# Last stage of a four-stage kernel: one block in place of two, rows kept apart from the bias adds, and two groups' column products issued ahead of the column weights

## The reference, cut to what matters

```python
def _L1_ffn_ref(x, col_emb, gate_w1, gate_b1, gate_w2, gate_b2, W_cols, b_cols, proj_w, proj_b, ln_g, ln_b):
    similarity = jnp.einsum('bsd,cd->bsc', _l2norm(x), _l2norm(col_emb))
    h = jax.nn.gelu(x @ gate_w1 + gate_b1, approximate=False)
    gate_values = jax.nn.sigmoid(h @ gate_w2 + gate_b2)
    logits = similarity + gate_values
    k = max(1, int(C * SPARSITY))                 # k = 1
    _, top_idx = jax.lax.top_k(logits, k)
    mask = jnp.sum(jax.nn.one_hot(top_idx, C, dtype=logits.dtype), axis=-2)
    weights = mask * jax.nn.softmax(logits, axis=-1)
    cols = jax.nn.gelu(jnp.einsum('bsd,cdn->bscn', x, W_cols) + b_cols, approximate=False)
    cols = cols * weights[..., None]
    combined = cols.reshape(Bq, Sq, -1)
    y = combined @ proj_w + proj_b + x
    mu = jnp.mean(y, axis=-1, keepdims=True)
    var = jnp.mean((y - mu) ** 2, axis=-1, keepdims=True)
    return (y - mu) * jax.lax.rsqrt(var + 1e-05) * ln_g + ln_b
...
x = x + jnp.tanh(g_ffn[1]) * _L1_ffn_ref(_layernorm(x, axis=-1), ...)
```

## Time and profile before

| | us |
|---|---|
| median of three runs (lowest to highest) | 1504.93 (1501.84 to 1507.17) |
| the profiled execution's own time | 1506.88 |
| its span from the first to the last instruction | 1505.1 |
| PE, DVE, ACT, POOL busy in the span | 1360.8, 1015.7, 620.0, 546.7 |
| last stage: first transposes of the gating start | 1184.8 |
| sigmoid starts, weights' transposes start | 1236.2, 1246.7 |
| second block's first matmul | 1252.9 |

### The profile page before, as it was taken

The page is one execution under the profiler, slowest core; times in us unless marked ns, Lnnn a source line. Parts: engine busy times, 40 slices in busy tenths (PEclk is TensorE's granted clock), DMA queues, the critical chain, the costliest instruction groups (busy, mean ns, idle before and its releaser), DMA issues. The chain is left out here.

```text
span 1505.1 us, 33126 instructions
## 1 busy us (share of the span) xinstructions
PE 1360.8 (90%) x12672; PEld 963.5 (64%) x12672; DVE 1015.7 (67%) x1961; ACT 620.0 (41%) x1371; POOL 546.7 (36%) x829
## 2 busy tenths in 40 slices
PE   3687999999999984899999999999999687999997
PEld 3464677777777762567776777667776463555555
DVE  6777665677556764778888888778888543444544
ACT  4433212211221112656666666656666442222221
POOL 0576888888840004323222232222231570000000
PEclk9998999999999996899999999999999688999999
DMA  8205445454531008667667777666672000000000
GB/s 243 66 1 171 132 134 165 124 165 133 162 110 41 32 1 117 123 83 95 84 85 92 97 96 91 84 83 84 84 93 24 0 1 0 13 12 12 20 17 25
DMA packets 92774, 120.25 MB, mean 80 GB/s; under 512 B 7414, under 2 KB 78899, under 8 KB 90348
## 3 DMA queue, kind: packets, MB, share of 16 engines
q1 hardware_dynamic: 83436, 87.82, 34.5%
q0 software_dynamic: 9216, 30.73, 7.0%
HBM read 96.42 MB, written 22.10 MB: 79 GB/s over the span
## 5 line engine op out<-in xcount | busy, mean ns | idle before, releaser
L1123 DVE TENSOR_REDUCE s_neg_max<-banks 112x1 bf16<-112x487 f32 x512 | 323.7, 662 | 92.5 <-PE banks L1234 89.3
L1059 ACT ACTIVATE s_prob<-banks 128x448 f32<-128x448 f32 x512 | 265.9, 547 | 180.2 <-PE banks L1256 180.0
L640 DVE TENSOR_TENSOR s_m<-banks,s_base 128x512 f32<-128x512 f32 x256 | 164.6, 685 | 129.3 <-PE banks L794 129.1
L1234 PE MATMUL banks<-s_k_t,s_q_t 96*112 96x487 bf16 x512 | 198.5, 388 | 1.5 <-DVE s_neg_max L1123 1.5
L1256 PEld LDWEIGHTS banks<-s_q_t,s_k_t 112*128 112x128 bf16 x2048 | 143.4, 99 | 82.1 <-issue 33.9
L1256 PE MATMUL banks<-s_q_t,s_k_t 112*128 112x112 bf16 x2048 | 187.2, 214 | 3.7 <-issue 3.0
L794 PE MATMUL banks<-s_gate_sel,s_tw 64*128 64x256 f32 x1024 | 147.4, 408 | 0.9 <-DVE s_m L640 0.8
L1270 PE MATMUL banks<-s_prob,s_v 128*32 128x112 f32 (+1 forms) x4096 | 129.2, 265 | 7.7 <-issue 7.7
L834 PE MATMUL banks<-s_m,s_act_t 128*112 128x256 f32 x512 | 129.8, 389 | 5.9 <-DVE x_res L659 5.8
L817 PEld LDWEIGHTS banks<-s_x_t,s_m 128*128 128x128 f32 x1024 | 119.1, 192 | 21.2 <-issue 20.9
L817 PE MATMUL banks<-s_x_t,s_m 128*128 128x112 f32 x1024 | 130.5, 281 | 0.0
(11 more groups left out here) (257 smaller groups left out, 2182.7 us busy)
## 6 DMA issues: line engine op xcount, KB each, us to landing
k_parts<-s_k_split POOLq DMA_DIRECT2D x64, 281.2 KB, 3.4
s_k_t<-k_parts SPq DMA_DIRECT2D x32, 562.5 KB, 7.7
s_tw<-in_tw SPq DMA_DIRECT2D x16, 1024.0 KB, 5.1
s_k_raw<-in_ctx_k POOLq DMA_DIRECT2D x64, 187.5 KB, 3.6
s_k_t<-k_parts SPq DMA_DIRECT2D x32, 375.0 KB, 9.9
s_v_raw<-in_ctx SPq DMA_DIRECT2D x32, 256.0 KB
s_src<-in_ctx SPq DMA_DIRECT2D x8, 896.0 KB, 14.4
s_k_t<-k_parts SPq DMA_DIRECT2D x32, 187.5 KB, 11.2
```

The lines of the kernel that those rows point to most:

```text
L640: nc.vector.tensor_tensor(dst[:, :, :, rows_], got, base[:, :, rows_].unsqueeze(2).broadcast_to([P, 2, B, HR]), ALU.add).then_inc(S["merge ...
L1059: nc.scalar.activation(prob[t % 2][:, c, :], w.bank(SCORE + n % SRING, P, TILE), ACT.Exp, scale=DH ** -0.5).then_inc(S["exp_done"], 1)
L1123: nc.vector.tensor_reduce(neg_max[half][:, ROWS + h, 0:1], w.bank(MAX + n % MRING, T, NKEY), AX.X, ALU.max, negate=True).then_inc(S["max_d ...
L1234: nc.tensor.matmul(w.bank(MAX + n % MRING, T, NKEY), q_t[k][0:ROWS, h, :], k_t[k][0:ROWS, h, FIRST:FIRST + NKEY], start=True, stop=True).t ...
```

## The change

`stage4` becomes one block with one set of semaphores, and the gating's loop over the groups is written out eight times.

- **Rows.** The norm writes straight to `xn`, which holds all 32 batches, and waits for nothing of POOL. POOL adds `proj_b` in `xn` in place, once PE has transposed the batch. Its adds of `ln_b` to `x_res` come after all of these: batches 0 to 15 at once, 16 to 31 once the weights are done.
- **Order at the start.** The norm's own root comes first, the columns' norm after the first group; the root of the columns is taken before the first group's PSUM copies on ACT, the copy of the columns' transposes goes from ACT to DVE, and the scaling of `ln_g` and `ln_b` comes after the second group's norm.
- **Two groups ahead.** After the gating PE computes the column products of groups 0 and 1 without their weights, over four banks for the Gelus (`ahead`); ACT writes the Gelu to `weighted`. The weights' transposes come group by group (`weights`), between the products of group 1, each with the spread of one turn of group 0. DVE multiplies in place (`weigh_ahead`). Then PE spreads group 1's weights, with the output of group 0 between, and groups 2 to 7 run as before.
- **Weights.** The softmax's factor (`total`, 32 values per partition) is split into three bf16 parts instead of the 512 weights, and one multiplication by the mask makes all parts.

```diff
+            @block.gpsimd
+            def _(pool):
+                pool.wait_ge(w.columns_in, N_COLUMNS)
+                for b in range(B):
+                    wait(pool, "x_tr", b + 1)
+                    nc.gpsimd.tensor_tensor(xn[:, b, :], xn[:, b, :], proj_b[:], ALU.add).then_inc(S["kept"], 1)
+                wait(pool, "biased", 1)
+                for b in range(B):
+                    if b == B // 2:
+                        wait(pool, "wts_done", 1)
+                    wait(pool, "xn_done", b + 1)
+                    nc.gpsimd.tensor_tensor(w.x_res[:, b, :], w.x_res[:, b, :], ln_b[:], ALU.add).then_inc(S["x_biased"], 1)
...
             @block.scalar
+                evacuate(0)
+                wait(act, "radicand_done", 3)
+                nc.scalar.activation(root[:], sumsq[:], ACT.Sqrt).then_inc(S["root_done"], 1)
+                nc.scalar.activation(table[:], cgate1_b[:], ACT.Gelu)
...
+                nc.scalar.activation(logit[:], logit[:], ACT.Exp).then_inc(S["soft_done"], 1)
+                nc.scalar.activation(table[:], cgate1_b[:], ACT.Gelu)
+                def ahead_gelu(g, j):
+                    wait(act, "ahead_ps", J4 * g + j + 1)
+                    nc.scalar.activation(weighted[g][:, j, :], w.bank(AHEAD_BANKS[j % 4], P, GT), ACT.Gelu,
+                                         bias=b_cols[:, j:j + 1]).then_inc(S["ahead_gelu"], 1)
+                for j in range(J4):
+                    ahead_gelu(0, j)
+                for g in range(0, NG, 2):
+                    wait(act, "wts_ps", g + 1)
+                    nc.scalar.activation(wts_t[:, g * GT:(g + 1) * GT], w.bank(2)[0:3 * C4, 0:GT], ACT.Copy)\
+                        .then_inc(S["wts_even"], 1)
+                    ahead_gelu(1, g)
+                    ahead_gelu(1, g + 1)
...
             @block.vector
+                def norm(i):
+                    for r in range(GB):
+                        b = GB * i + r
+                        normalised(nc, w, xn[:, b, :], b).then_inc(S["xn_done"], 1)
+                norm(0)
...
-                    chain.link(nc.vector.tensor_tensor(val[:], logit[:], eq[:], ALU.mult))
-                    chain.link(nc.vector.tensor_tensor(val[:], val[:], each(total), ALU.mult))
-                    chain.link(nc.vector.tensor_copy(parts[:, :, 0, :], val[:]))
-                    chain.link(nc.vector.tensor_tensor(val[:], val[:], parts[:, :, 0, :], ALU.subtract))
-                    chain.link(nc.vector.tensor_copy(parts[:, :, 1, :], val[:]))
-                    nc.vector.tensor_tensor(parts[:, :, 2, :], val[:], parts[:, :, 1, :], ALU.subtract)\
-                        .then_inc(S["wts_done"], 1)
+                chain.link(nc.vector.tensor_copy(total3[:, :, 0], total[:]))
+                chain.link(nc.vector.tensor_tensor(total[:], total[:], total3[:, :, 0], ALU.subtract))
+                chain.link(nc.vector.tensor_copy(total3[:, :, 1], total[:]))
+                chain.link(nc.vector.tensor_tensor(total3[:, :, 2], total[:], total3[:, :, 1], ALU.subtract))
+                nc.vector.tensor_tensor(parts[:], eq[:].unsqueeze(2).broadcast_to([T, B, 3, C4]),
+                                        total3[:].unsqueeze(3).broadcast_to([T, B, 3, C4]), ALU.mult)\
+                    .then_inc(S["wts_done"], 1)
+                def weigh_ahead(g, j):
+                    n = J4 * g + j
+                    wait(dve, "ahead_gelu", n + 1)
+                    wait(dve, "spread_ps", n + 1)
+                    bank = (6 if g == 0 else 2) + j % 2
+                    nc.vector.tensor_tensor(weighted[g][:, j, :], weighted[g][:, j, :], w.bank(bank, P, GT),
+                                            ALU.mult).then_inc(S["weighed_ahead"], 1)
+                for g in range(1, NG, 2):
+                    wait(dve, "wts_ps", g + 1)
+                    nc.vector.tensor_copy(wts_t[:, g * GT:(g + 1) * GT], w.bank(3)[0:3 * C4, 0:GT]).then_inc(S["wts_odd"], 1)
+                    weigh_ahead(0, g - 1)
+                    weigh_ahead(0, g)
...
             @block.tensor
+                    if i == 0:
+                        turn_columns()
+                        wait(pe, "col_t_done", 1)
...
+                def ahead(g, j):
+                    n = J4 * g + j
+                    wait(pe, "ahead_gelu", n - 3)
+                    for kk in range(KD):
+                        last = nc.tensor.matmul(w.bank(AHEAD_BANKS[j % 4], P, GT), w_cols[:, kk, j * P:(j + 1) * P],
+                                                x_t[:, kk, g * GT:(g + 1) * GT], start=(kk == 0), stop=(kk == KD - 1))
+                    last.then_inc(S["ahead_ps"], 1)
...
+                wait(pe, "x_g_done", B)
+                for j in range(J4):
+                    ahead(0, j)
+                weights(0)
+                for j in range(J4):
+                    ahead(1, j)
+                    if j + 1 < NG:
+                        weights(j + 1)
+                    spread(0, j)
...
+                wait(pe, "ahead_gelu", 2 * J4)
+                for j in range(J4):
+                    spread(1, j)
+                    if j == 1:
+                        wait(pe, "weighed_ahead", J4)
+                    if j % 2:
+                        output(0, 0, j // 2)
+                wait(pe, "weighed_ahead", 2 * J4)
                 turns(turn, pe)
```

More of the change, by code:

```diff
@@ new lines, in stage4 @@
+        tmp, root, var = sb("s4_tmp", [T, B]), sb("s4_root", [T, B]), sb("s4_var", [T, B])
+        table = sb("s4_table", [P, 1])
+        ident16 = sb("s4_ident16", [T, T], BF16)
+        parts = sb("s4_parts", [T, B, 3, C4], BF16)
+        x_g = [sb(f"s4_x_g{k}", [P, GB, KD, T]) for k in range(2)]
+        sumsq = sb("s4_sumsq", [T, B])
+        inv_norm = sb("s4_inv_norm", [T, B])
+        hid = sb("s4_hid", [P, GT])
+        logit, gate, eq, val = (sb("s4_" + n, [T, B, C4]) for n in ("logit", "gate", "eq", "val"))
@@ L1628, in turns @@
                 chain.loop(NG // 2 - 1, 2 * per, two)
-            turn(NG - 1, 1, True, NG // 2 - 1)
         with nc.Block() as block:
@@ new lines, in _ @@
+                evacuate(0)
+                wait(act, "radicand_done", 3)
+                nc.scalar.activation(root[:], sumsq[:], ACT.Sqrt).then_inc(S["root_done"], 1)
+                nc.scalar.activation(table[:], cgate1_b[:], ACT.Gelu)
+                for i in range(NG):
+                    if i + 1 < NG:
+                        evacuate(i + 1)
+                    wait(act, "hid_ps", i + 1)
+                    nc.scalar.activation(hid[:], w.bank(2, P, GT), ACT.Gelu, bias=cgate1_b[:]).then_inc(S["hid_done"], 1)
@@ L1664, in _ @@
             def _(dve):
-                chain = Chain(dve, S["chain2"])
+                chain = Chain(dve, S["chain"])
+                nc.vector.tensor_scalar(var[:], w.mean_var[:, :, 1], EPS, None, ALU.add).then_inc(S["radicand_done"], 1)
+                wait(dve, "root_done", 1)
+                chain.link(inverse_root(nc, chain, w.rstd[:, :, 0], root[:], var[:], tmp[:]))
+                def norm(i):
+                    for r in range(GB):
+                        b = GB * i + r
+                        normalised(nc, w, xn[:, b, :], b).then_inc(S["xn_done"], 1)
@@ new lines, in _ @@
+                norm(1)
+                wait(dve, "root_done", 2)
+                wait(dve, "radicand_done", 2)
+                chain.link(inverse_root(nc, chain, col_inv[:], col_root[:], col_ss[:], col_tmp[:]))
+                nc.vector.tensor_scalar(col_emb[:], col_emb[:], col_inv[:], None, ALU.mult).then_inc(S["col_n_done"], 1)
+                wait(dve, "root_done", 3)
+                wait(dve, "radicand_done", 3)
+                chain.link(inverse_root(nc, chain, inv_norm[:], root[:], sumsq[:], tmp[:]))
@@ new lines, in _ @@
+                chain.link(nc.vector.tensor_tensor(val[:], eq[:], col_less[0:T, :].unsqueeze(1).broadcast_to([T, B, C4]),
+                                                   ALU.mult))
+                chain.link(nc.vector.tensor_reduce(low[:], val[:], AX.X, ALU.min))
+                chain.link(nc.vector.tensor_tensor(eq[:], val[:], each(low), ALU.is_equal))
+                wait(dve, "soft_done", 2)
+                chain.link(nc.vector.tensor_reduce(total[:], logit[:], AX.X, ALU.add))
+                chain.link(nc.vector.reciprocal(total[:], total[:]))
```

363 lines of the change are left out of this document (149 added, 214 removed).

## The result

The changed kernel takes 1490.12 us (median of 20 runs, 1475.58 to 1500.03) against 1507.51 us for the kernel before (20 runs, 1499.11 to 1520.92). The medians lie 17.4 us apart. The ratio, for which the two slowest runs of the changed kernel are left out, is 0.9872, with a 95% interval of 0.9853 to 0.989, which is 19.3 us less (16.6 to 22.2). Forecast were 18.5 us less and 1486.4 us. Most of the difference in the absolute number is the point from which it was reckoned: the kernel before was at 1504.9 in its first three runs and is at 1507.5 over twenty.

What follows compares the result with a forecast made beforehand. Only PE's idle or half-clock time before 1257 in the last stage could be won, POOL pacing the gating. 6.1 us by the gating plus 12.4 from there to group 2 make 18.5: 1504.9 to 1486.4 us, range 1479 to 1495.

Steps and rivals of the forecast that it cites:

- the likeliest case: The prediction's own forecast for the whole kernel: 1486.4 us, own range 1483 to 1490, chance 0.55.
- The start: Last stage's start: first transposes 3.0 us earlier, first hidden product at 1187.0 in place of 1192.54, 5.5 us gained.
- the bound of POOL's price taken at half: Start: chain and second four norms take 2.2 us free to 5.2 beside POOL; about half was taken.
- The columns' wait in group 0: Gating's first group: new wait for the columns' transposes and DVE copy, 1.5 us (0.8 to 2.8), group lasting 7.9.
- The six groups: Rest of the gating: two groups at 6.1 us, four at 4.61, 30.6 in all, 2.1 less than before.
- The contention of POOL and DVE: Softmax: POOL's `ln_b` adds delay three DVE products by 0.45 us each, 1.4 in all (0 to 2.1).
- The half clock behind the idle time: After the gating: one stretch at half clock behind PE's idle 2 us adds 0.8 us.
- From the weights' transposes to group 2: First weights 0.4 us, rounds of 2.5, then last Gelu, spreads and outputs, from G + 14.4 to G + 51.4.
- The split and the other 16 adds: Weights 1.1 us earlier, hidden behind products; POOL's other 16 adds end near G + 24, before group 0 finishes.
- the rival that nothing covers: Rounds with product, transposes and spread are serial, 4.2 us each in place of 2.5; 1501 us and more, chance 0.03.

Runs made afterwards that it cites:

- after_again: The changed kernel as it is, run once more: 1490.92 us, ratio to before 0.9886.
- pool_late: Changed kernel with all 32 of POOL's `ln_b` adds waiting for the weights, not only the second 16: 1486.52 us, ratio to before 0.9848.
- pool_all: Changed kernel with none of POOL's `ln_b` adds waiting for the weights, 32 in a row: 1503.35 us, ratio to before 0.9958.
- old_split: Changed kernel with the weights split over all 512 values again, as before: 1489.33 us, ratio to before 0.9857.
- ahead_late: Changed kernel with PE waiting for the weights before group 0's first product, so nothing covers the softmax: 1499.84 us, ratio to before 0.9948.
- pool_quarter: Changed kernel with only 8 of POOL's `ln_b` adds ahead of the weights, not 16: 1480.93 us, ratio to before 0.9806.
- pool_late_warm: pool_late plus three idle matmuls on PE, ahead of the first and second transposes: 1479.31 us, ratio to before 0.9825.

## Why the prediction was right, point by point

The total was right (19.3 us measured, 18.5 forecast; 1490.12 in the range of 1479 to 1495, just above the likeliest case's own 1483 to 1490). Its terms were less so, and that the total came out so near is in part luck: by the steps of the traces the last stage gained less than forecast, 15.0 to 16.7 us with the mean gating (worked out at the end of this section).

| step, us into the last stage | before | forecast | after | after_again |
|---|---|---|---|---|
| first transposes | 6.2 | 3.2 | 3.3 | 3.3 |
| first hidden product | 14.0 | 8.4 | 8.6 | 8.6 |
| second | 20.3 | 16.3 | 17.1 | 16.0 |
| eighth | 53.1 | 46.9 | 50.5 | 45.8 |
| end of the gating, G | 57.1 | 51.0 | 54.4 | 49.7 |
| fifth product | | G + 8.2 | G + 11.2 | G + 11.2 |
| weights' first transposes | 68.1 | G + 14.4 | G + 20.3 | G + 20.1 |
| group 2's first spread | 121.7 | G + 52.2 | G + 55.8 | G + 55.6 |

**The start** was right to 0.3 us: the first transposes, and the bound of POOL's price taken at half. The products beside POOL's `proj_b` adds took 0.67 and 0.65 us, as in the earlier trace rows.

**The columns' wait in group 0** was there but shorter than forecast (1.5 us, 0.8 to 2.8), and the sum came out by the clock. Group 0 lasts 8.5 and 7.4 us in the two traces of the changed kernel, where 7.9 was forecast. PE's wait for the columns' copy is 1.0 us in these waits of after (PE's idle time in this group is 0.97 us, in after_again 0.35), and the clock in the window of group 0 is 0.70, before 0.77:

```profile
PE banks L1662 <- DVE s_xn L109: 2.0, 1, 2.0
...
PE banks L1691 <- DVE s_col_t L1538: 1.0, 1, 1.0
```

**The six groups** were right in the mean and wrong for a single trace. Forecast was the eighth at 46.9, with two of six groups at 6.1 us for a stretch at half clock. Ten traces with the same gating have it at 50.5, 45.8, 45.8, 43.9, 45.8, 45.8, 50.8, 47.2, 43.9 and 50.8, 47.0 in the mean. The six groups take 30.3 us in the mean, forecast 30.6, by a somewhat other sum: the last one at full clock takes 3.81 and not 4.61, so the clock costs 3.4 us and not 3.0. No norm waits for POOL any more. That the clock falls beside a busy PE is confirmed: it was 0.52 from 1194.02 to 1202.56, behind more than 6 us without a gap.

**The contention of POOL and DVE is the step that failed.** I took 0.45 us for each pair of instructions and 1.4 us in all, with 2.1 as the upper end. It cost 4.24, twice that end. The mistake was in the model, not in the number: both bounds supposed that DVE and POOL take turns, instruction by instruction, as the earlier trace rows can be read. Against this row of adds DVE got no turn. The price of the product was the rest of POOL's row, which was in my reach: I had worked out that 4.6 us of POOL fall on the softmax. The Trainium skill, "SBUF — State Buffer", section "SBUF: two separate sides", says that of a DVE instruction with two SBUF inputs and a GpSimd one that reads SBUF whichever starts first keeps the shared ports for its whole instruction, and the other is blocked. One whole add for each of three products was 2.1 us in my sum, and the measured 4.24, seven adds on one product, disagrees. Its section "Who interferes with whom" says that a DVE instruction with one SBUF operand doesn't contend, its two-port modes aside, and this the traces do bear out. Of these two products of a bank with `s_weighted` in after, the first lies beside POOL's second row (1239.48 to 1250.44), the second doesn't:

```profile
1248.37 0.60 DVE L1588 TENSOR_TENSOR s_weighted<-s_weighted,banks 128x448 f32<-128x448 f32 x1
...
1252.96 0.60 DVE L1588 TENSOR_TENSOR s_weighted<-s_weighted,banks 128x448 f32<-128x448 f32 x1
```

Turn by turn is still what other rows show, and they narrow down what is open. The kernel before has a row of POOL adds in its gating that start 0.68 us apart, as close as the `ln_b` adds (0.68), and there DVE's products of 112x32 wait for one add each (the first one stands in the earlier trace rows):

```profile
1192.53 0.72 POOL L1418 TENSOR_TENSOR x_res<-x_res,s_ln_b 112x256 f32 x1
1193.21 0.72 POOL L1419 TENSOR_TENSOR s_xn<-s_xn_g,s_proj_b 112x256 f32 x1
1193.89 0.72 POOL L1418 TENSOR_TENSOR x_res<-x_res,s_ln_b 112x256 f32 x1
1194.00 0.66 DVE L104 TENSOR_TENSOR s_inv_norm<-s_inv_norm,s_tmp 112x32 f32<-112x32 f32 x1
1194.57 0.72 POOL L1419 TENSOR_TENSOR s_xn<-s_xn_g,s_proj_b 112x256 f32 x1
```

So neither the closeness of the adds nor the size of the product separates the two cases. What does wasn't found.

**The half clock behind the idle time** was the second error in size. I counted 0.8 us for an idle 2.0; it was 4.91 us idle, and the four products behind it took 9.12 (8.90 in after_again) in place of 6.28: 2.8 us. With 0.67 us idle it was nothing (pool_late), and with 15.79 us it was 3.0 (9.31 in pool_all). The Trainium skill, "TensorE: Matmul & The Clock Gate", section "Why this matters for your kernels", advises against idle gaps between bursts of matmuls. Behind this gap the trace agrees. By the same rule the gating, without gaps, should have run at full clock, as the prediction worked out, and there the trace does not agree (0.52 from 1194.02).

**What made up for it.** From the weights' transposes to group 2 the forecast had 37.0 us without the half clock. Measured are 35.5: the first weights and eight rounds take 18.9 instead of 20.0 (a round 2.30, not 2.5), and the spreads and outputs behind them 16.6 instead of 17.0. Together: 3.0 later by the Gelu, 2.1 more than the 0.8 for the clock, 1.5 less behind: G + 55.8 for G + 52.2.

**The split and the other 16 adds** cost and gain nothing, as forecast: old_split has the same times, and with all 32 adds behind the weights (pool_late) it is still 35.5 us from the weights' transposes to group 2. And the rival that nothing covers is refuted: a round takes 2.30 us and not 4.2, and ahead_late shows 9 us for the overlap. (That rival was priced at 1500 by its own sum and stated as 1501 and more.)

Two things stay open. By the steps the last stage gained 11.4 us in one pair of traces and 18.0 in the other, and 15.0 or 16.7 with the mean of ten for the gating (311.5 against 326.5 or 328.2); the timing says 16.6 to 22.2. The rest may lie in the untouched stages: they end at 1179.2 in the mean of the two traces of before and at 1176.0 in the mean of the twelve others, 3.2 less, but those twelve alone spread over 16 us. The traces are too few to say whether that is chance. And which of pool_late, pool_quarter and pool_late_warm is best isn't settled; pool_late, run twice, and the other two lie 3.6 to 10.8 us below the change in their medians, and in the traces of all three the stretch behind the gating is 7.1 us shorter than in the changed kernel's, at the softmax and the products behind it.

## What to carry to other kernels

Where work is moved off one engine's critical wait, look at what it lands beside: here the rows part gained some 10 us in the gating and gave back 7 in the softmax, since it moved a row of POOL's adds onto a DVE product with both operands in SBUF. Take what is left of the other engine's whole row as the upper bound of such a meeting (here it was the price), and let the row start behind the serial chain (one changed number in a wait). And compare steps, counted from the start of their own stage: two single profiles of one kernel differed by more than most parts of this change.

## What the hardware showed that was not expected

- A DVE product whose two operands lie in SBUF waited for all of POOL's ready adds: 4.93 us beside 16 adds in a row, 15.82 beside 32, 5.17 for a product of only 112x32. A product of 112x32 takes only 0.65 beside the `proj_b` adds at the stage's start (four in a row of 2.77 us), and beside the adds of the kernel before. In all these rows the adds start 0.68 us apart, so a gap between them is not the reason; what is stays open.
- The same code in the same stage meets another clock in each execution: the eighth hidden product starts between 43.9 and 50.8 us in ten traces. From the second hidden product on PE was busy without a gap in each of them. What decides it wasn't found.
- An idle PE is paid twice: 4.91 us without work were followed by 2.8 us of slower products.
